# First batch of a two-layer state-space stage with seven states by rows, its turn of dt u through one PSUM bank, and a third buffer of silu products in an FP4 feed-forward

## The reference

```python
# block 0, feed-forward (I = 352): every operand rounded to FP4 in blocks of 16
gate = fp4_linear(x, w_gate); y = fp4_linear(x, w_up)
h = jax.nn.silu(gate) * y
return fp4_linear(h, w_down)

# block 1, one Mamba layer (inner width 256, 16 states, 512 steps)
dA = jnp.exp(dt[..., None] * A)
dBu = dt[..., None] * Bm[:, :, None, :] * u[..., None]
def step(h, xs):
    dA_t, dBu_t, C_t = xs
    h = dA_t * h + dBu_t
    y = jnp.einsum('bdn,bn->bd', h, C_t)
    return (h, y)
```

## Time and profile before

| | |
|---|---|
| median of 3 runs | 809.49 us (808.19 to 809.61) |
| the profiled execution: its own time | 809.59 us |
| its span, first to last instruction | 807.8 us |
| mean granted PE clock | 0.883 |
| busy: PE, DVE, ACT, POOL | 654.5, 596.9, 487.1, 440.4 us |
| feed-forward, from the first L1475 to the end of the last L1460 | 74.0 to 151.9 us |
| layer 0, first scan; layer 1, first scan | 203.9 us; 442.7 us |
| end of layer 1's last scan | 636.2 us |
| from there to the end (gates, router, experts) | 171.6 us |

### The profile page before, as it was taken

The page is one execution under the profiler, slowest core; times in us unless marked ns, Lnnn a source line. Parts: engine busy times, 40 slices in busy tenths (PEclk is TensorE's granted clock), DMA queues, the critical chain, the costliest instruction groups (busy, mean ns, idle before and its releaser), DMA issues. The chain is left out here.

```text
span 807.8 us, 9052 instructions
## 1 busy us (share of the span) xinstructions
PE 654.5 (81%) x3043; PEld 402.3 (50%) x3043; DVE 596.9 (74%) x802; ACT 487.1 (60%) x904; POOL 440.4 (55%) x246
## 2 busy tenths in 40 slices
PE   4847666597799998989987798999989960699993
PEld 2344444432455555545432554555545450688883
DVE  6795775464699999999845799899998859544331
ACT  3552332377799787878567998888877551222321
POOL 1236553100398888878500598879877524044636
PEclk9975788596599999999997699999999955799998
DMA  5000000000233233323101123222222261012213
GB/s 186 0 3 1 0 1 0 1 2 8 76 88 96 91 90 92 91 81 103 27 4 55 42 91 99 82 92 89 90 84 93 74 239 52 2 17 24 25 16 27
DMA packets 30333, 47.15 MB, mean 58 GB/s; under 512 B 3512, under 2 KB 12104, under 8 KB 29776
## 3 DMA queue, kind: packets, MB, share of 16 engines
q1 hardware_dynamic: 25600, 44.45, 17.4%
q0 software_dynamic: 4688, 2.13, 3.0%
HBM read 42.07 MB, written 4.49 MB: 58 GB/s over the span
## 5 line engine op out<-in xcount | busy, mean ns | idle before, releaser
L465 POOL TENSOR_TENSOR hc_all<-hs_all,c_row 128x1024 f32<-128x1024 f32 x88 | 207.2, 2364 | 140.1 <-DVE hs_all L1573 139.8
L1099 PE MATMUL ps<-hc_all,ident 128*128 128x512 f32 x512 | 237.5, 600 | 2.9 <-DVE y_sb L1549 1.8
L1573 DVE TENSOR_TENSOR_SCAN hs_all<-da,ps 128x1024 f32<-128x1024 f32 x88 | 198.5, 2273 | 23.3 <-ACT da L763 11.6
L763 ACT ACTIVATE da<-big,a_neg 128x511 f32<-128x511 f32 x256 | 169.8, 711 | 56.7 <-DVE w_ffn L1573 46.9
L1099 PEld LDWEIGHTS ps<-hc_all,ident 128*128 128x128 f32 x512 | 91.0, 193 | 88.5 <-issue 76.6
L465 POOL TENSOR_TENSOR hc_all<-w_ffn,c_row 128x1024 f32<-128x1024 f32 x40 | 94.6, 2365 | 39.6 <-DVE w_ffn L1573 37.6
L1573 DVE TENSOR_TENSOR_SCAN w_ffn<-da,ps 128x1024 f32<-128x1024 f32 x40 | 91.4, 2286 | 3.6
L519 POOL DMA_INDIRECT out<-hc_all,hs_all x32 | 49.6, 1549 | 52.2 <-issue 31.9
L1122 PE MATMUL ps<-ident,dbu 128*128 128x128 f32 x432 | 59.1, 282 | 11.5 <-DVE w_ffn L1573 4.4
L1122 PEld LDWEIGHTS ps<-ident,dbu 128*128 128x128 f32 x432 | 51.2, 145 | 25.8 <-issue 10.8
L1564 DVE TENSOR_TENSOR ps<-big,ps 128x1024 f32<-128x1024 f32 x48 | 58.1, 1211 | 0.2
(11 more groups left out here) (279 smaller groups left out, 1046.5 us busy)
## 6 DMA issues: line engine op xcount, KB each, us to landing
c_row<-c_rows SPq DMA_DIRECT2D x128, 256.0 KB, 3.1
tmpA<-w_in SPq DMA_DIRECT2D x2, 1024.0 KB, 7.4
tmpB<-w_in SPq DMA_DIRECT2D x2, 1024.0 KB, 9.5
x_tok<-x_in SPq DMA_DIRECT2D x2, 512.0 KB, 5.7
out<-x_tok SPq DMA_DIRECT2D x1, 1024.0 KB, 11.4
xm_rows<-xn SPq DMA_DIRECT2D x1, 1024.0 KB, 5.1
w_mod<-w_mod_in SPq DMA_DIRECT2D x2, 384.0 KB, 6.5
w_ffn<-w_ffn_in SPq DMA_DIRECT2D x1, 560.0 KB, 7.6
```

The source lines that it names most:

```text
L465: nc.gpsimd.tensor_tensor(hc[:, n % 4, :, :], hs3[HS_BUF[n]].rearrange("p (i s) -> p i s", i=IC), c_row[:, n % 4, :].unsqueeze(1).to_broad ...
L763: ins = nc.scalar.activation(da[:, n % 2, i, 1:S], dtT[:, b, i, 1:S], ACT.Exp, scale=a_neg[:, l, i, n:n + 1])
L1099: mm = nc.tensor.matmul(ps[:, YS + i, :], ident[:], hc[:, n % 4, i, :], start=(n == 0), stop=(n == NS - 1))
L1573: v.tensor_tensor_scan(hs3[HS_BUF[n]], decay, pair.rearrange("p i s -> p (i s)"), 0.0, ALU.mult, ALU.add).then_inc(c_scan, 1)
```

## The change

1. `BY_ROW` becomes a list per batch: state 1 is by row in the first batch of each layer, so there are seven states by row there and nine by token; the other batches keep six and ten.
2. In the first batch both halves of dt u are turned through bank `OUT`, like those of the others. PE does the first half, the row of state 1, then the second half; ACT copies the first half, does `magnitude(B - 1)`, copies the second. The product ahead of the loop is gone.
3. `softplus_ln` waits for both turned halves at `(b > 1) == i` instead of `b > 1 and i`.
4. `hid` has three buffers. Product `p` waits for the transposes of pair `p-3`, and `add_down(p - 3)` follows it; the last three adds come behind the last rounding.

```diff
-        hid = tmpB[:, 0:4 * FF].rearrange("p (h t f) -> p h t f", h=2, t=2)
+        hid = tmpB[:, 0:6 * FF].rearrange("p (h t f) -> p h t f", h=3, t=2)
...
-        BY_ROW = [0, 2, 5, 8, 11, 14]
-        BY_TOKEN = [n for n in range(NS) if n not in BY_ROW]
+        BY_ROW = [[0, 1, 2, 5, 8, 11, 14] if g % B == 0 else [0, 2, 5, 8, 11, 14] for g in range(L * B)]
+        BY_TOKEN = [[n for n in range(NS) if n not in rows] for rows in BY_ROW]
...
                 def softplus_ln(b, i):
-                    if b > 1 and i:
+                    if (b > 1) == i:
                         act.wait_ge(c_turned, IC * (l * B + b))
...
                         if b == 0 and n == 0:
                             turned(0, 0)
+                            magnitude(B - 1)
                             turned(0, 1)
-                            for m in range(AHEAD):
-                                if m in BY_TOKEN:
-                                    product(0, m)
-                            magnitude(B - 1)
...
                 def turn(b, i):
                     pe.wait_ge(q["m_dtu"], b + 1)
-                    if b == 0:
-                        pe.wait_ge(b_ready, l + 1)
-                    else:
-                        pe.wait_ge(c_turned, IC * (l * B + b) + i)
-                        after(pe, c_h, l * B + b - 1)
+                    after(pe, c_turned, IC * (l * B + b) + i)
+                    after(pe, c_h, l * B + b - 1)
                     for t in range(TB):
-                        mm = nc.tensor.transpose(ps[:, OUT if b else TURN + i, t * P:(t + 1) * P], dtuT[:, b, i, t * P:(t + 1) * P], ident[:])
+                        mm = nc.tensor.transpose(ps[:, OUT, t * P:(t + 1) * P], dtuT[:, b, i, t * P:(t + 1) * P], ident[:])
...
                 turn(0, 0)
-                turn(0, 1)
                 pe.wait_ge(diag_ready, 1)
                 for b in range(B):
                     for n in range(NS):
-                        if n + 1 in BY_ROW:
+                        if n + 1 in BY_ROW[l * B + b]:
                             row(b, n + 1)
                         elif n + 1 == NS and b + 1 < B:
                             row(b + 1, 0)
-                        if n in BY_TOKEN:
+                        if b == 0 and n == 0:
+                            turn(0, 1)
+                        if n in BY_TOKEN[l * B + b]:
                             increment(b, n)
...
             for pair in range(2 * B):
                 b = pair // 2
                 dve.wait_ge(f_silu, pair + 1)
-                after(dve, f_htr, pair - 1)
-                v.tensor_tensor(hid[:, pair % 2, :, :], silu_g[:, pair % 2, :, :], ps[:, UP:UP + 2, 0:FF],
+                after(dve, f_htr, pair - 2)
+                v.tensor_tensor(hid[:, pair % 3, :, :], silu_g[:, pair % 2, :, :], ps[:, UP:UP + 2, 0:FF],
                                 ALU.mult).then_inc(f_hid, 1)
+                if pair >= 3:
+                    add_down(pair - 3)
                 dve.wait_ge(f_hid, pair + 1)
                 after(dve, q_h["q_done"], pair - 1)
                 scales(q_h, hid_flat(pair), 1 + pair % 2)
...
                 if pair:
                     round_hidden(pair - 1)
-                if pair >= 2:
-                    add_down(pair - 2)
                 if pair % 2 == 0 and b + 1 < B:
                     round_fp4(q_x, b + 2, x_flat(b + 1), mag_x)
             round_hidden(2 * B - 1)
-            add_down(2 * B - 2)
-            add_down(2 * B - 1)
+            for pair in range(2 * B - 3, 2 * B):
+                add_down(pair)
```

More of the change, by code:

```diff
@@ L148, in hid_flat @@
         def hid_flat(pair):
-            return hid[:, pair % 2, :, :].rearrange("p t f -> p (t f)")
+            return hid[:, pair % 3, :, :].rearrange("p t f -> p (t f)")
         w_in = sb("w_in", [P, L, 2 * DI])
@@ L205, in upto @@
         def upto(of, b, n):
-            return len(of) * b + sum(m <= n for m in of)
+            return sum(map(len, of[:b])) + sum(m <= n for m in of[b])
         def since(buf, n):
@@ L644, in _ @@
                 after(act, q_h["q_rounded"], pair)
-                magnitudes(q_h, pair, hid[:, pair % 2, :, :], ps[:, MAG:MAG + 2, 0:FF])
+                magnitudes(q_h, pair, hid[:, pair % 3, :, :], ps[:, MAG:MAG + 2, 0:FF])
                 if pair % 2 and b + 2 < B:
@@ L754, in _ @@
                     for n in range(AHEAD):
-                        if b and n in BY_TOKEN:
+                        if b and n in BY_TOKEN[l * B + b]:
                             product(b, n)
@@ L984, in transpose_hidden @@
                     for k, n in enumerate(KD):
-                        mm = nc.tensor.transpose(ps[0:n, HIDT + j, k * P:(k + 1) * P], hid[:, pair % 2, j, k * P:k * P + n],
+                        mm = nc.tensor.transpose(ps[0:n, HIDT + j, k * P:(k + 1) * P], hid[:, pair % 3, j, k * P:k * P + n],
                                                  ident[:])
@@ L1188, in _ @@
                     back(1)
-                    pe.wait_ge(c_bm, len(BY_ROW) * L * B)
+                    pe.wait_ge(c_bm, sum(map(len, BY_ROW)))
                     back(2)
@@ L1356, in round_hidden @@
                 dve.wait_ge(q_h["q_mag"], pair + 1)
-                buf, mag = hid[:, pair % 2, :, :], ps[:, MAG:MAG + 2, 0:FF]
+                buf, mag = hid[:, pair % 3, :, :], ps[:, MAG:MAG + 2, 0:FF]
                 rounded = mag_h[:, pair % 2, :].rearrange("p (t f) -> p t f", t=2)
@@ L1558, in _ @@
                         pair = ps[:, INC[n % 2]:INC[n % 2] + IC, :]
-                        if n in BY_ROW:
+                        if n in BY_ROW[l * B + b]:
                             if n == 0:
```

8 lines of the change are left out of this document (4 added, 4 removed).

## The result

| | before | after |
|---|---|---|
| median of 15 runs (lowest to highest) | 809.49 us (807.51 to 811.07) | 803.91 us (802.82 to 809.07) |
| ratio after / before, 95% interval | | 0.9953 [0.9938, 0.9969] |
| the profiled execution: its time, span | 809.59, 807.8 us | 802.82, 800.9 us |
| mean granted PE clock | 0.883 | 0.890 |
| PE, DVE, ACT, POOL busy | 654.5, 596.9, 487.1, 440.4 us | 650.4, 597.8, 483.3, 440.3 us |

Faster, and by more than forecast (1.7 us): the ratio gives 3.8 us, the two medians 5.6. Two later comparisons gave 0.9960 [0.9938, 0.9983] and 0.9962 [0.9944, 0.9981].

A forecast was written before the change was run, and what follows sets the result against it. DVE was taken to set the pace in each layer's first batch. Layers -3.0 us and feed-forward +1.3 us gave -1.7 us from 809.59, so 807.9, or 807.8 us for the median; range 805.8 to 811.0 us.

The forecast's parts named there:

- What bounds the first batch: Layers' first batch: DVE sets the pace, so shifting its early scans shifts the layer's end.
- rival C: Layers: they absorb the shift and only the feed-forward's +1.3 us stays, total 810.8 us; chance 0.10.
- The states of the first batch: State 1 by row in each layer's first batch: scan 1 starts 1.5 us earlier, -3.0 us over both layers.
- One bank is free: First batch's turns: the second waits for the first copy, done at 207.43, before 207.8, so the wait costs nothing.
- The row's multiply is covered: DVE before scan 1: the added multiply, 1.22 us, falls inside the 5.89 us wait for state 1's decay.
- Three buffers, +1.3 us: Feed-forward stage: 0.9 us gained up to pair 7, 2.2 us lost in the tail, bounds +0.5 to +1.6.
- Rival A: Layers: PE's clock rises later and scan 4 comes late; 811.5 us for a rise 4 us later; chance 0.13.
- Rival B: Feed-forward: gate and up of pair 4 or 6 run at the upper clock, 1.9 us earlier, total 805.9 us; chance 0.12.

The follow-up runs named there:

- e6: e4 with the first batch's turns in two banks, both ahead of state 1's row, and both copies ahead of the magnitude; 804.10 us.
- e4: The changed kernel with three buffers of products kept but the adds of the down projections at their old places; 805.32 us, ratio 0.9912 to before.
- e3: The changed kernel again, unchanged; 810.5 us, ratio 0.9960 to before.
- e1: The changed kernel without the feed-forward part (two buffers of products, adds at their old places); 807.54 us, ratio 0.9934 to before.
- e11: e4 once more, unchanged, beside the changed kernel on one chip; 803.97 us, ratio 0.9879 to before.
- e12: The changed kernel once more, unchanged, on the same chip as e11; 810.38 us, ratio 0.9962 to before.
- e2: The kernel before with the feed-forward part of the change alone; 812.21 us, ratio 0.9994 to before.
- e7: The changed kernel with pair 5's add moved between the two last roundings instead of behind both; 803.89 us, stage 76.39 us.
- e8: e4 with 15 unread transposes of the unit matrix where PE waits behind product 7; 803.11 us, product 7 to last add 14.94 us.

## Why the prediction was wrong

- **What bounds the first batch**: right. The shift of scan 1 went through in full (181.51 and 181.52 us behind it), so rival C falls. DVE's wait before scan 1 fell to 2.56 us (2.9 was forecast).
- **The states of the first batch**: right in mechanism, mis-sized. The step "scan 1 starts at 211.9 instead of 213.37: 1.5 us a layer" measured 2.05 and 2.03, outside my own bounds (1.2 to 1.7). From scan 0 the forecast is 8.01 us and the result 7.43. Of the 0.58 us the first copy's place is 0.17, which the change doesn't account for. The other 0.41 are sums of durations: rows of one engine that waited for nothing overlap, each started about 0.1 us before the last one's end (0.09 to 0.11 us in the rows of DVE and ACT above, 0.21 and 0.08 in the first ones of PE). So the turns came 0.9 to 1.0 us apart and not 1.06, and the second copy 1.86 us after the first instead of 2.02 (0.16); the starts of the exponential and the decay came 0.20 earlier in the same way, and the scan 0.05. The magnitude helped: it started behind the first half of DVE's positive part (205.90, inside 204.83 + 1.39), not behind all of it, and filled the 0.27 us of idle time between the copies, which I had booked as a possible loss. At ACT's decay the overlap is 0.10 us (the exponential ends at 207.75 + 1.06 = 208.81, and the decay starts at 208.71), and my sum had left it out.
- **One bank is free**: right (e6 against e4, together with the magnitude's place). **The row's multiply is covered**: right (206.27, inside the old hole).
- **Three buffers, +1.3 us**: wrong in size, in both terms. The loop up to product 7 was to gain 0.9 us. It took 57.45 to 58.56 us in the four traces with the change and 60.05 and 59.65 in the two without, 1.85 less on the mean and between 1.1 and 2.6 from pair to pair of traces. The tail was to lose 2.2 us and lost 1.84 in the first trace; all four traces have 19.66 us, where the others have 17.82 and 17.75. The tail's miss is again the sum of durations: product and add started 0.80 us apart, not 0.89, and the transposes of pair 6 began 7.83 us behind product 7, not 8.15. Such overlaps are too small for the loop's miss. In e3, against the kernel before, 0.30 us of it stands already at product 2, which comes at 13.61 us from the first product there, at 13.91 before, and at 13.54 and 13.94 in e1 and e11, so it is no work of the buffer. Another part is gate and up of pair 6, 4.19 us in the first trace, 4.32 in e12 and 5.06 in e2 and e3. How much the buffer itself gained in the loop beyond 0.9 us stays open. What moves the stage was right: e4 and e7 show the buffer's gain and the adds' two prices.
- **Rival A** (PE's clock rises later in the layers) didn't occur: no scan waits, and the clock stood at 1.00 when state 4's increment began. That work of PE brings the clock up, and a pause keeps it down (the case for A and against B), was my estimate: the earlier trace rows hold one rise and not its cause. e8 tested it: with 15 more transposes the tail's clock was 0.89, without them (e4) 0.56. **Rival B**: its sign, a shorter stage, did appear, by 0.76 us in the first trace, but not in e2 and e3. Gate and up of pair 6 took 4.19 us (granted clock 0.62) and those of pair 4 5.06 (0.50) in that first trace, against 2.61 at the upper clock (1.00) in the earlier trace rows, so 0.9 of the 1.9 us that B had meant, and for pair 6 alone.
- **The time**: 807.8 us was forecast and 803.91 measured, below the range. The layers are worth about 4.1 us and the feed-forward stage nothing that shows, which gives 805.4, already below the range's 805.8 (which stands for B's sum, 805.9). The ratio's 3.8 us hold no more than that. The remaining 1.5 us of the medians are put down to the clock, by the stretches named above; that is argued from one trace of each kernel and not shown for the medians. On the later chips the medians' distance was 2.4 and 2.8 us.

## What to carry to other kernels

Work out an engine's chain from start to start of its rows, not from sums of durations: over five instructions it was 0.4 us a layer here. When a buffer is added to remove a wait, look at what was moved along with it: here the moved adds gave back all of the buffer's 3.5 us, and the kernel that kept the adds in place was the better one. And look for idle time of the late engine itself: ACT's decay of state 1 was late by its queue alone and fitted into 4 us that ACT spent waiting.
